# The gate of a two-of-eight expert layer: 17 VectorE steps become 14, with a new order of the expert stage

## What is computed

```python
router_probs = softmax(x @ router_w + router_b)          # 8 experts
top_p, top_i = top_k(router_probs, 2)
top_p = top_p / sum(top_p)
expert_out = einsum('bnd,edc->bnec', x, expert_w) + expert_b
out = einsum('bnk,bnkc->bnc', top_p, gathered(expert_out, top_i))
x = t + out                                              # x inside is ln_t(t)
```

## Time and profile before

| | |
|---|---|
| median of three runs | 1282.1 us (1280.45 to 1282.62) |
| the profiled execution | 1280.34 us |
| its span, first to last instruction | 1278.5 us |
| granted TensorE clock, mean | 0.996 |
| instructions | 30756 |

### The profile page before, as it was taken

One profiled execution on the slowest core, in us unless ns is written; L12 is line 12 of the kernel. 1 busy time (PEld: TensorE's weight loads), 2 busy tenths in 40 slices (PEclk: granted clock), 3 DMA queues, 4 the chain that ended last, 5 costly groups with the idle time before them and its releaser, 6 DMA issues.

```text
span 1278.5 us, 30756 instructions
## 1 busy us (share of the span) xinstructions
PE 1253.2 (98%) x10991; PEld 1152.0 (90%) x10991; DVE 746.1 (58%) x1614; ACT 532.3 (42%) x1433; POOL 531.5 (42%) x654
## 2 busy tenths in 40 slices
PE   7999999999999899999999999999999999999997
PEld 5999999999999899999999999999777777777775
DVE  5666666455555322222222222243999999999997
ACT  6455555344444322222210000130666767676763
POOL 1354554000000000000014444454788888888886
PEclk9999999999999899999999999999999999999999
DMA  4122222000000000000001222111002010101011
GB/s 163 54 68 66 73 75 85 1 0 0 0 0 0 1 0 0 0 0 0 0 16 53 69 69 69 47 60 35 2 8 99 28 53 28 53 28 53 28 54 53
DMA packets 15835, 47.60 MB, mean 37 GB/s; under 512 B 2960, under 2 KB 3472, under 8 KB 15760
## 3 DMA queue, kind: packets, MB, share of 16 engines
q1 hardware_dynamic: 15616, 46.28, 10.7%
q10 hardware_dynamic: 144, 0.33, 0.1%
HBM read 31.86 MB, written 14.75 MB: 36 GB/s over the span
## 4 chain that ended last, share of the span: by engine, by line
PE 96%; DVE 2%; ACT 1%; issue 1%; DMA 0%; DVEq 0%; ACTq 0%
PE twin L1179 36%; PE twin L1053 29%; PE twin L1217 13%; PE twin L1234 7%; PE twin L1154 5%; PE twin L1170 3%; PE twin L1092 2%; PE twin L1073 0%; DVE scratch L998 0%; DVE act_buf L1006 0%; PE twin L1080 0%; DMA x_in<-x 0%; DVE spare L998 0%; DVE tnum L784 0%; ACT spare L697 0%
## 5 line engine op out<-in xcount | busy, mean ns | idle before, releaser
L1179 PE MATMUL twin<-kbuf,late 128*128 128x136 f32 (+2 forms) x3940 | 459.6, 280 | 5.0 <-DVE kbuf L899 5.0
L1179 PEld LDWEIGHTS twin<-kbuf,late 128*128 128x128 f32 x3940 | 458.5, 192 | 5.3 <-DVE kbuf L899 5.3
L1053 PE MATMUL twin<-parts 128*128 128x384 f32 (+2 forms) x2070 | 380.6, 343 | 3.7 <-DVE act_buf L770 2.2
L1053 PEld LDWEIGHTS twin<-parts 128*128 128x128 f32 x2070 | 368.2, 189 | 7.1 <-DVE act_buf L770 2.9
L962 DVE SCALAR_TENSOR_TENSOR kbuf<-twin,act_buf 128x144 f32<-128x144 f32 x394 | 121.3, 308 | 333.4 <-PE twin L1179 333.4
L422 POOL TENSOR_TENSOR act_buf<-kbuf,x_in 128x144 f32 (+1 forms) x140 | 68.5, 490 | 523.6 <-DVE kbuf L962 523.6
L1217 PE MATMUL twin<-em,parts 64*128 64x512 f32 x1350 | 213.8, 421 | 1.4 <-ACT spare L697 0.9
L645 ACT ACTIVATE act_buf<-kbuf 128x144 f32 x196 | 63.2, 323 | 166.8 <-DVE kbuf L962 166.8
L1217 PEld LDWEIGHTS twin<-em,parts 64*128 64x128 f32 x1350 | 112.0, 187 | 22.4 <-issue 8.3
L660 ACT ACTIVATE squares<-twin 128x384 f32<-128x384 f32 (+1 forms) x81 | 37.9, 468 | 209.8 <-PE twin L1154 208.0
L797 DVE SCALAR_TENSOR_TENSOR act_buf<-twin,act_buf 128x400 f32 (+1 forms) x70 | 40.2, 575 | 75.3 <-PE twin L1053 51.9
(11 more groups left out here) (123 smaller groups left out, 1571.0 us busy)
## 6 DMA issues: line engine op xcount, KB each, us to landing
x_in<-x_col SPq DMA_DIRECT2D x20, 720.0 KB, 4.1
result<-act_buf SPq DMA_DIRECT2D x34, 400.0 KB, 3.0
scratch<-x_tok SPq DMA_DIRECT2D x8, 448.0 KB, 3.3
spare<-x_tok SPq DMA_DIRECT2D x8, 448.0 KB, 3.4
scratch<-x_tok SPq DMA_DIRECT2D x8, 384.0 KB, 3.1
spare<-x_tok SPq DMA_DIRECT2D x8, 384.0 KB, 3.1
x_in<-x SPq DMA_DIRECT2D x3, 400.0 KB, 5.1
x_in<-x SPq DMA_DIRECT2D x2, 200.0 KB, 4.0
```

The source lines that it names most:

```text
L1053: last = mm(acc[:, lo:hi], vw[:, k, wpart, si], carry[:, cpart, g, lo + s * BG:hi + s * BG], start=first and si == 0, stop=final and si == ...
L1179: last = mm(banks[CONV[g]][:, lo * BG:hi * BG], hw[:, k, si], kbuf[:, g, lo + s:hi + s].rearrange("p j b -> p (j b)"), start=si == 0, stop ...
```

## The change

The gate has 14 steps on VectorE in place of 17. The bias is added to the logits by GpSimd, behind the last `scale_tokens` of a region (`s_bl`), with `bias_row` now in SBUF. The denominator 1+exp(gap) and its reciprocal leave VectorE: ScalarE computes ln(exp(gap)+1) and exp(-that), behind its exponential (`s_el`, `s_iv`). In even regions tile 1 is now an act tile, tile 4 a copy tile, and tile 2, a copy tile before, is a whole tile. All order tables but the row of `TURN_AT` for chunks 0 to 2 are new.

```diff
--- before.py
+++ after.py
@@ -102,7 +102,8 @@
         eb = sb("eb", [P, E * C + E])
 
         em = sb("em", [P, 2, E * C], F32R)
-        best = sb("best", [P, 3, NG])
+        best = sb("best", [P, 4, NG])
+        bias_row = sb("bias_row", [P, E])
 
         twin = [ctx.enter_context(nc.psum_tensor(f"twin{i}", [P, 2, 512], F32)) for i in range(4)]
         banks = [twin[i // 2][:, i % 2] for i in range(8)]
@@ -113,10 +114,11 @@
         FLIP = [2, 1]
         SUMS, LOG, CTB = [4, 5], 6, 7
         PREP = [6, 7]
+        EM_READY = 9
         EARLY_CT, EARLY_TB = [2, 3, 7], [4, 5]
 
-        ACT_TILES = [(4, 6), (4, 6)]
-        COPY_TILES = [(0, 1, 2, 5, 10, 11, 12), (0, 1, 2, 5, 10, 11)]
+        ACT_TILES = [(1, 6), (4, 6)]
+        COPY_TILES = [(0, 4, 5, 10, 11, 12), (0, 1, 2, 5, 10, 11)]
         LAST_ACT, LAST_COPY, LAST_WHOLE = (1, 4, 7, 9), (), (3, 6, 11)
         TERMS = [(0, 0), (0, 1), (1, 0)]
         LAG = 3
@@ -188,8 +190,6 @@
                        if any(j * REG < (t + 1) * TN and t * TN < (j + 1) * REG for t in REGIONS[r][lo:hi]))
             return group_no(last[0]) + last[1] + 1
 
-        bias_row = banks[LOG][:, 2 * NSM + 3 * NG:2 * NSM + 3 * NG + E]
-
         def stage_of(n):
 
             k = n % (2 * BLOCK)
@@ -226,28 +226,28 @@
             return not isinstance(n, int) or n > 0
 
         NCST = 4 + E + 3 + 1
-        SMN = 17
-        GAP_STEP = 8
-        EX_STEP = 12
-
-        TURN_AT = [[(7, 1), (8, 1), (9, 1), (10, 2), (12, 1)],
-                   [(7, 1), (8, 1), (9, 1), (10, 2)]]
-        COPY_AT = [[(7, 1), (8, 0), (9, 1), (11, 0), (11, 1)],
-                   [(7, 0), (8, 0), (10, 0), (11, 0)]]
-        VAR_AT = [[(8, 1), (8, 2), (9, 2), (11, 2), (12, 2)],
-                   [(8, 0), (8, 2), (9, 2), (11, 0)]]
-        INV_AT = [[(9, 1), (9, 1), (10, 0), (12, 1), (12, 1)],
-                   [(8, 0), (8, 1), (11, 1), (11, 1)]]
-        SCALE_AT = [[(9, 0), (9, 1), (10, 1), (12, 1), (12, 1)],
-                   [(9, 0), (11, 0), (11, 1), (11, 1)]]
-        BACK_AT = [[(0, 2), (2, 2), (3, 2), (5, 1)],
-                   [(1, 2), (3, 0), (3, 2), (5, 1), (6, 1)]]
-        HIGH_AT = [[(1, 0), (2, 0), (4, 0), (5, 0)],
-                   [(1, 0), (3, 0), (3, 0), (5, 0), (5, 1)]]
-        LOW_AT = [[(1, 1), (3, 0), (3, 2), (5, 2)],
-                   [(2, 0), (3, 0), (4, 0), (5, 1), (6, 1)]]
-        STEP_AT = [[(2, 2), (3, 1), (4, 0), (4, 2), (5, 1), (6, 0), (7, 0), (8, 0), (8, 1), (9, 1), (10, 0), (11, 0), (11, 0), (11, 1), (11, 2), (12, 1), (12, 2)],
-                   [(2, 1), (2, 2), (3, 0), (3, 2), (4, 0), (4, 2), (5, 2), (6, 1), (6, 2), (8, 0), (9, 0), (9, 1), (9, 2), (10, 2), (11, 0), (11, 2), (11, 2)]]
+        SMN = 14
+        GAP_STEP = 7
+        EX_STEP, INV_STEP = 11, 13
+
+        TURN_AT = [[(7, 1), (8, 1), (9, 1), (11, 0), (12, 1)],
+                   [(7, 1), (8, 1), (9, 1), (11, 0)]]
+        COPY_AT = [[(8, 0), (8, 0), (10, 0), (11, 0), (11, 1)],
+                   [(7, 1), (8, 1), (9, 0), (10, 1)]]
+        VAR_AT = [[(8, 0), (8, 1), (10, 0), (11, 2), (12, 2)],
+                   [(7, 2), (8, 1), (10, 2), (11, 1)]]
+        INV_AT = [[(10, 0), (10, 0), (11, 0), (12, 1), (12, 1)],
+                   [(8, 1), (9, 0), (11, 0), (11, 1)]]
+        SCALE_AT = [[(9, 0), (10, 1), (11, 1), (12, 1), (12, 1)],
+                   [(7, 1), (8, 1), (10, 1), (11, 1)]]
+        BACK_AT = [[(0, 2), (2, 2), (4, 0), (5, 2)],
+                   [(1, 2), (3, 0), (4, 0), (5, 1), (6, 1)]]
+        HIGH_AT = [[(0, 1), (2, 1), (3, 0), (5, 1)],
+                   [(1, 0), (3, 0), (3, 0), (4, 1), (5, 1)]]
+        LOW_AT = [[(2, 0), (3, 0), (3, 1), (6, 0)],
+                   [(1, 2), (2, 2), (4, 0), (6, 0), (6, 1)]]
+        STEP_AT = [[(3, 0), (4, 0), (4, 1), (5, 1), (7, 2), (8, 0), (8, 2), (9, 2), (10, 1), (10, 2), (11, 1), (12, 1), (12, 2), (12, 2)],
+                   [(2, 1), (3, 0), (3, 2), (4, 0), (5, 0), (6, 0), (7, 0), (7, 2), (8, 1), (9, 1), (9, 2), (10, 2), (11, 1), (11, 1)]]
         S0 = 2 * W - 2 - 28
         FRONTS = [(0, c) for c in range(NCH[0])] + [(1, c) for c in range(NCH[1])]
         TURN_STEP = [0, 1, 2, 3, 4, 9, 10, 11, 12]
@@ -256,8 +256,8 @@
         SCALE_STEP = [2, 3, 4, 5, 6, 11, 12, 13, 14]
         LOW_STEP = [5, 6, 7, 8, 9]
         GATE_STEP = [(8, 0), (9, 0), (10, 1), (11, 1), (12, 1), (13, 1), (14, 0), (14, 1), (15, 0), (15, 1), (16, 0), (16, 1),
-                     (17, 0), (17, 1), (18, 0), (18, 1), (19, 0)]
-        EXP_AT = [(11, 0), (7, 1)]
+                     (17, 0), (18, 0)]
+        EXP_AT = [(11, 1), (8, 0)]
 
         def at(table, p, place):
 
@@ -316,7 +316,10 @@
         s_th = sem("s_th")
         s_tl = sem("s_tl")
         s_sm = sem("s_sm")
+        s_bl = sem("s_bl")
         s_ex = sem("s_ex")
+        s_el = sem("s_el")
+        s_iv = sem("s_iv")
         s_p = sem("s_p")
         s_g = sem("s_g")
         s_ga = sem("s_ga")
@@ -438,10 +441,18 @@
                     pool.wait_ge(s_cp, n + 1)
                     pool.wait_ge(s_r2, n + 1)
                     if c == 0 and r > 0:
-                        pool.wait_ge(s_sm, (r - 1) * SMN + 1)
+                        pool.wait_ge(s_bl, r)
                     nc.gpsimd.tensor_tensor(lg, xl, inv.to_broadcast([P, k, 2, E]), ALU.mult)
                 if half != 0:
                     nc.gpsimd.tensor_tensor(xn, xn, inv.to_broadcast([P, k, 2, C]), ALU.mult).then_inc(s_xn2, 1)
+                    if c == NCH[r] - 1:
+                        ng = 2 * NT[r]
+                        pool.wait_ge(s_em, EM_READY)
+                        pool.wait_ge(s_xn2, n + 1)
+                        if r > 0:
+                            pool.wait_ge(s_sm, (r - 1) * SMN + 2)
+                        nc.gpsimd.tensor_tensor(logit[:, 0:ng], raw_logit[:, 0:ng], bias_row[:, :].unsqueeze(1).to_broadcast([P, ng, E]),
+                                                ALU.add).then_inc(s_bl, 1)
 
             UNROLLED = (S0 - W + 1) // (2 * COLS) * 2
 
@@ -681,6 +692,10 @@
             def exponential(r):
                 act.wait_ge(s_sm, r * SMN + GAP_STEP)
                 act.activation(best[:, 1], best[:, 0], ACT.Exp).then_inc(s_ex, 1)
+                act.wait_ge(s_ex, r + 1)
+                act.activation(best[:, 3], best[:, 1], ACT.Ln, bias=1.0).then_inc(s_el, 1)
+                act.wait_ge(s_el, r + 1)
+                act.activation(best[:, 2], best[:, 3], ACT.Exp, scale=-1.0).then_inc(s_iv, 1)
 
             def gate_odd(r, p):
 
@@ -837,7 +852,7 @@
             for q in range(2):
                 half = slice(q * C, (q + 1) * C)
                 nc.vector.tensor_copy(cl_w[half, P + q * E:P + (q + 1) * E], ew[half, E * C:]).then_inc(s_em, 1)
-            nc.vector.tensor_copy(bias_row, eb[:, E * C:]).then_inc(s_em, 1)
+            nc.vector.tensor_copy(bias_row[:, :], eb[:, E * C:]).then_inc(s_em, 1)
             dve.wait_ge(s_em, 8)
             nc.vector.tensor_tensor(em[:, 1], ew[:, 0:E * C], em[:, 0].bitcast(F32), ALU.subtract).then_inc(s_em, 1)
             with dve.Fori(1, HP // 2 - 1) as i:
@@ -923,10 +938,9 @@
                 gap, ex, inv = (best[:, k, 0:ng] for k in range(3))
                 work = banks[LOG][:, 0:2 * NSM].rearrange("p (k n e) -> p k n e", k=2, e=E)[:, :, 0:ng]
                 small = banks[LOG][:, 2 * NSM:2 * NSM + 3 * NG].rearrange("p (k n) -> p k n", k=3)[:, :, 0:ng]
-                m1, idx, den = (small[:, k] for k in range(3))
+                m1, idx = (small[:, k] for k in range(2))
                 rank, lg, ht, fi = rank_w[:, 0:ng], logit[:, 0:ng], hit[:, 0:ng], first[:, 0:ng]
                 return [
-                    lambda: v.tensor_tensor(lg, raw_logit[:, 0:ng], bias_row.unsqueeze(1).to_broadcast([P, ng, E]), ALU.add),
                     lambda: v.tensor_reduce(m1, lg, AX.X, ALU.max),
                     lambda: v.tensor_tensor(work[:, 0], lg, spread(m1, ng), ALU.subtract),
                     lambda: v.scalar_tensor_tensor(ht, work[:, 0], 0.0, rank, ALU.is_equal, ALU.mult),
@@ -938,8 +952,6 @@
                     lambda: v.scalar_tensor_tensor(ht, work[:, 1], 0.0, rank, ALU.is_equal, ALU.mult),
                     lambda: v.tensor_reduce(idx, ht, AX.X, ALU.max),
                     lambda: v.tensor_tensor(work[:, 0], rank, spread(idx, ng), ALU.is_equal),
-                    lambda: v.tensor_scalar(den, ex, 1.0, None, ALU.add),
-                    lambda: v.reciprocal(inv, den),
                     lambda: v.tensor_tensor(work[:, 1], work[:, 0], spread(ex, ng), ALU.mult),
                     lambda: v.tensor_tensor(work[:, 0], work[:, 1], fi, ALU.add),
                     lambda: v.tensor_tensor(gate[q][:, 0:ng], work[:, 0], spread(inv, ng), ALU.mult),
@@ -948,9 +960,11 @@
             def softmax(r, k):
 
                 if k == 0:
-                    dve.wait_ge(s_xn2, chunk_no(r) + NCH[r])
+                    dve.wait_ge(s_bl, r + 1)
                 elif k == EX_STEP:
                     dve.wait_ge(s_ex, r + 1)
```

(2 more changed lines are left out.)

## The result

| | before | after |
|---|---|---|
| median of six runs each (us) | 1281.08 | 1287.69 |
| lowest and highest (us) | 1280.45, 1282.62 | 1284.51, 1288.22 |
| profiled execution (us) | 1280.34 | 1287.60 |
| its span (us) | 1278.5 | 1285.4 |

The account below looks back on a forecast made before the run. TensorE was taken as the bound, VectorE right behind it. Terms -2.1 - 0.2 + 3.5 + 1.0 + 1.8 = +4.0 us gave 1284.3 us profiled, 1286.1 us as median; range 1280.5 to 1289.5 us.

Parts of the forecast that it names:

- A: The forecast itself: the three late `add_out` appear about as computed; 1286.1 us, chance 0.50.
- D: Worse: late TensorE delays later gatings, including ScalarE's of tile 1; 0.3 us more per region pair, 1288.5 us, chance 0.08.
- tile 3: Even regions 2 to 14: full tile 2 ahead of `add_out` delays the sum's load by 0.53 us; +3.5 us.
- tile 10: Regions 4 to 14: a gate step ahead of `add_out` makes the sum's load 0.16 us late; +1.0 us.
- Shorter sums: Even regions 0 to 14: one sum of 16 less, one of 8 more, saving 0.26 us each; -2.1 us.
- Ends of regions 1 and 3: At tile 11, the gate's last two steps move ahead of `add_out`, 0.9 us later at two places; +1.8 us.
- GpSimd, costed at nothing: One bias addition per region, estimated at 0.54 us, with GpSimd 5.8 us of 43 free; no cost.
- ScalarE at nothing: Two more small activations per region, with ScalarE 13 us of 43 free; no cost.
- VectorE's relief in the tail: Region 16, where region 17's gate is computed: less VectorE work saves 0.2 us, between 0.5 and 0.
- B: Faster: `add_out` reaches TensorE in time because VectorE starts tile 2's gating earlier; 1279.3 us, chance 0.13.
- C: No change: the wait at tile 3 comes, the other late `add_out` don't; 1283.3 us, chance 0.27.
- E: GpSimd's 18 additions each block VectorE for 0.54 us, costing 9.7 us; 1295.8 us, chance 0.02.

Follow-up runs that it names:

- Run 10: Changed kernel with GpSimd's bias addition done twice; 1292.64 us, ratio 1.0087.
- run 5: Changed kernel with the old kinds of tiles and the gate's last two steps in odd regions behind `add_out` again; 1281.29 us, ratio 0.9998.
- run 3: Kernel before with only the new 14-step gate (bias on GpSimd, logarithm and exponential on ScalarE), old kinds and order; 1283.63 us, ratio 1.0019.
- run 6: As run 3, but GpSimd adds the bias for regions 2 to 17 behind its work on tile 0 of the next region; 1280.98 us, ratio 0.9995.
- run 1: Changed kernel with the kinds of tiles of the kernel before; 1285.15 us, ratio 1.0030.
- runs 2 to 9: Eight follow-ups: two with edited tables of the changed kernel, six putting the new gate, new kinds or full tiles into the kernel before; 1278.61 to 1284.23 us.

## Why the prediction was right, and where it was not

The side and the range held, and of the cases the mechanism of A. The size is in part luck. The forecast was 4.0 us above the median before and 6.0 were measured, which is nearer to the time of D (+6.4) than to that of A. Two terms that were too large (tile 3 and tile 10, 1.6 us together) offset about as much as the clock's fall added, which the sum had left out. Term by term, for the profiled executions (+4.0 forecast, +7.3 measured, of which 6.8 lie in the span):

- **Shorter sums,** -0.26 us in an even region: measured -0.28. Right.
- **Tile 3,** +0.53 us: the load came where I had put it (1.1 us behind the experts, released by `add_out`), and the matmuls lost 0.42, between the lower bound of 0.30 and the 0.53 taken. Right in kind, a fifth too large: the load now runs only 0.03 us ahead of its matmuls (1077.12 to 1077.15), where it ran 0.19 ahead before (1070.76 to 1070.95), and this lead is used up first.
- **Tile 10,** +0.16 us, six times: the load is 0.10 late and TensorE 0.00. The step that failed here was that every late load is a late matmul. A load that runs ahead of its matmul can be a little late for free.
- **Ends of regions 1 and 3,** +0.9 us each: measured 0.93 twice. The chain behind it was right to 0.02 us: I had `add_out` starting at 936.68, and it did at 936.70 in the old time.
- **The clock at region 4:** +1.5 us that no term of mine had. It is the largest error. I had looked at the granted clock of steady stretches alone, never asked what a longer idle time does to it. Run 10's trace, with the same wait, doesn't have it.
- **Tile 6 of regions 1 and 3:** +0.3 and +0.4 us, where the `channels` matmuls now wait for the second part of the split (two waits, up to 0.5 us). I had not looked at this wait; run 5 has it too.
- **Single places:** the account has five more steps of 0.2 to 0.3 us, 1.2 in all, that no term had: tiles 3 and 7 of region 0, tile 7 of region 2, tile 3 of region 3 and tile 4 of region 13. At tile 7 of region 0 TensorE waits for the `add_out` of a group of three tiles (the row below); the others are not followed up.

```profile
902.49 0.46 PE L1248 MATMUL twin<-ident,more 64*128 64x64 f32 x8 [0.20 <-DVE act_buf L1020]
```

- **GpSimd, costed at nothing:** in the changed kernel this came out, in even regions, but my reason was wrong. "The first of those sums is read three tiles later" was never held against rows; the row would have shown it ending with `add_out`, so the wait at tile 3 that I called `add_out`'s was GpSimd's as well. On the old tables the addition costs the 0.53 us in each of six regions (3.2 us) of run 3, which run 6 gets back. In the changed kernel the earlier multiplications of the new `SCALE_AT` make room for it (run 5), and the late `add_out` gives even regions 0.4 us on top (run 10). One of my signs of being wrong, GpSimd among those that release TensorE, did appear in the brackets of the weight loads, and there it took the distances to tell that it was `add_out` in even regions and GpSimd, without a cost, in odd ones.
- **ScalarE at nothing:** right (run 6).
- **VectorE's relief in the tail, -0.2:** not seen; from region 16 to the end the account adds 0.1.
- The first 0.75 us lie ahead of the expert stage. The other kernels have between 0.3 and 1.7 us there, with runs that hardly differ in that part, so I do not count it to the change.

Of the rivals, B fell at the gating of tile 2, which started when TensorE allowed it, as I had said. C falls with the 0.93 us at the ends of regions 1 and 3. D's mechanism isn't seen: a pair of regions loses 0.16 us, and TensorE's waits for ScalarE are the two of before, 0.9 us. E is out: GpSimd's additions take 0.60 us and VectorE's gatings kept their 0.68 to 0.69. The Trainium skill ("SBUF — State Buffer", "SBUF: two separate sides") limits the lock to VectorE instructions with two inputs in SBUF or in a two-port mode. The trace agrees as far as it goes: in run 3 `add_out`, with one input in SBUF, took its 0.68 us at 1071.64 beside GpSimd's addition (1071.44 to 1072.04).

What stays open: why the clock falls at region 4 and not at region 2 behind the same idle time, and where it falls in the executions without a profile. These have only a mean. It is 0.994 in all seven of run 1, whose trace has the fall, but also in 33 of 73 of the kernel before, whose trace has none at region 4.

## What to carry to other kernels

List everything that an instruction waits for and write down when each part of it ends. Here two engines were done within 0.02 us of each other at the load that starts a group. Taking 1 us off VectorE was worth nothing by itself; giving work to either cost most of its length (0.42 of 0.53 us, 0.53 of 0.60). For GpSimd the loss went when the addition, or the work ahead of it, was moved. A tile that costs one engine less may stand where the other has room (tile 5) but not in front of what the bound engine waits for (tile 2), and it pays to choose the places one by one.

## What was new about the hardware

TensorE was idle for 1.64 to 1.65 us at six such places in the traces of the changed kernel, run 1 and run 10. Behind four of them (region 2 in all three, region 4 in run 10) the granted clock stayed at 1.00; behind two (region 4 in the changed kernel and in run 1) it fell to 0.50. The fall came while TensorE was busy again, within 2 us of its first matmul, and cost 1.5 us, more than the 0.93 us of added waiting ahead of it. Where TensorE waited for 0.43 to 0.72 us at the start of region 4, in the kernel before and runs 2 to 9, the clock stayed at 1.00. A longer wait can so cost more than twice what it adds. DMA traffic behind the wait isn't what decides: in run 10 there was as much of it (a share of 0.82), behind the same 1.65 us:

```profile
986.00:988.00 2.00, 2.00 (x32) 1.59 (x30) 0.51 (x2) 0.85 (x3) 1.79 (x3) 1.00 0.82 328
```

GpSimd's addition with a broadcast operand takes 0.60 us for 192 elements a partition and 0.63 for 208 (region 9 of the changed kernel). A line through 0.271 for 48 and 0.832 for 384 gives 0.51 and 0.54. Two that depend on each other start 0.68 us apart (run 10).
